# A convolution, attention and routed-expert kernel: filters on a semaphore of their own, filter places filled by three engines, the last logits in two parts

## The reference, cut to what matters

```python
x = x + conv(group_norm(x), bias, up_filter, dn_filter)   # per channel: upsample 2x, 12x12 filter,
                                                          # leaky relu * sqrt(2), 12x12 filter, keep every 2nd
t = tokens(x)                                             # 16 sequences of 1024 tokens, 32 wide
t = t + attention(layer_norm(t), Wq, Wk, Wv)              # causal softmax, one head
t = t + ffn(layer_norm(t), gate_w, gate_b, weight1, weight2)
# ffn: logits of 16 experts per token; softmax over the 1024 tokens of an image; each expert takes its
# 8 strongest tokens, pools them with their weights, two dense layers with gelu, and adds the result
# back to the tokens it took
out = images(t)
```

## Time and profile before

| | |
|---|---|
| median of 3 runs | 413.75 us (411.68 to 414.61) |
| the profiled execution's own time | 406.51 us |
| its span | 404.6 us |
| PE busy | 348.4 us (86%) |
| DVE busy | 310.3 us (77%) |
| ACT busy | 256.4 us (63%) |
| POOL busy | 239.8 us (59%) |
| mean granted TensorE clock | 0.943 |

### The profile page before, as it was taken

One profiled execution on the slowest core, in us unless ns is written; L12 is line 12 of the kernel. 1 busy time (PEld: TensorE's weight loads), 2 busy tenths in 40 slices (PEclk: granted clock), 3 DMA queues, 4 the chain that ended last, 5 costly groups with the idle time before them and its releaser, 6 DMA issues.

```text
span 404.6 us, 7839 instructions
## 1 busy us (share of the span) xinstructions
PE 348.4 (86%) x3046; PEld 260.4 (64%) x3046; DVE 310.3 (77%) x559; ACT 256.4 (63%) x343; POOL 239.8 (59%) x141
## 2 busy tenths in 40 slices
PE   1189998999899999999599999999986887969775
PEld 1068876667587776857477677676764535647574
DVE  2888779786969878699868786986998995765521
ACT  0113454797988959788476778898696888830500
POOL 5314564366679698886734989856497974162000
PEclk9999999999999999999789999999998997998755
DMA  3900000000000000000000000000020000000311
GB/s 105 203 1 2 2 0 2 2 3 0 3 3 2 0 2 3 2 1 2 0 2 2 2 2 2 2 2 2 0 56 0 2 0 25 19 0 20 86 52 53
DMA packets 16033, 6.70 MB, mean 17 GB/s; under 512 B 6735, under 2 KB 15869, under 8 KB 15997
## 3 DMA queue, kind: packets, MB, share of 16 engines
q1 hardware_dynamic: 13280, 5.55, 5.3%
q10 hardware_dynamic: 2717, 0.66, 1.1%
HBM read 3.63 MB, written 2.11 MB: 14 GB/s over the span
## 4 chain that ended last, share of the span: by engine, by line
PE 58%; DVE 15%; ACT 10%; issue 9%; DMA 3%; POOL 2%; SPq 1%; ACTq 1%; DVEq 0%; POOLq 0%
PE psB L874 13%; PE psA L874 11%; PE psB L989 5%; ACT Pp L582 5%; PE psA L974 4%; PE psB L1010 4%; PE psA L1018 3%; PE psA L1054 3%; DVE negmax L739 3%; PE psA L864 3%; PE psA L1032 2%; DVE Pp L393 2%; DVE xin L682 1%; PE psB L992 1%; ACT e L581 1%
## 5 line engine op out<-in xcount | busy, mean ns | idle before, releaser
L393 POOL TENSOR_TENSOR Pp<-e,Pp 128x1024 f16<-128x1024 f32 x45 | 107.3, 2393 | 11.7 <-ACT Pp L582 11.5
L739 DVE TENSOR_REDUCE negmax<-psA 128x1 f32<-128x512 f32 (+7 forms) x128 | 90.7, 749 | 18.5 <-PE psA L977 17.6
L581 ACT ACTIVATE e<-psB 128x1024 f32<-128x1024 f32 (+1 forms) x80 | 76.7, 958 | 9.9 <-PE psB L992 4.5
L582 ACT ACTIVATE Pp<-psB 128x1024 f16<-128x1024 f32 (+1 forms) x80 | 77.0, 963 | 0.0
L874 PE MATMUL psB<-xin,UU 128*128 128x224 f16 (+1 forms) x480 | 56.6, 277 | 1.1 <-ACT Pp L582 0.6
L974 PE MATMUL psA<-zK,yQ 128*128 128x512 f16 (+1 forms) x192 | 49.2, 340 | 9.0 <-DVE uT L759 4.9
L989 PE MATMUL psB<-yQ,zK 128*128 128x512 f16 (+1 forms) x192 | 49.2, 335 | 6.9 <-ACT Pp L582 3.7
L874 PE MATMUL psA<-y,DD 128*128 128x224 f16 (+1 forms) x480 | 55.1, 273 | 0.0
L874 PEld LDWEIGHTS psB<-xin,UU 128*128 128x128 f16 x480 | 47.1, 99 | 9.5 <-ACT oT L586 1.5
L874 PEld LDWEIGHTS psA<-y,DD 128*128 128x128 f16 x480 | 46.7, 98 | 5.5
L489 POOL TENSOR_TENSOR y<-y 128x1024 f16<-128x1024 f32 x16 | 36.7, 2291 | 14.1 <-ACT y L547 14.1
(11 more groups left out here) (157 smaller groups left out, 603.7 us busy)
## 6 DMA issues: line engine op xcount, KB each, us to landing
x_all<-in_x_dram SPq DMA_DIRECT2D x4, 512.0 KB, 4.6
out_dram<-x_all SPq DMA_DIRECT2D x8, 256.0 KB, 2.3
yQ<-rows SPq DMA_DIRECT2D x32, 2.0 KB
Pp<-filter_tables ACTq DMA_DIRECT2D x4, 121.9 KB, 3.3
w_halves<-y SPq DMA_DIRECT2D x12, 32.0 KB, 1.8
cst<-shape_constants SPq DMA_DIRECT2D x1, 326.5 KB, 4.2
y<-in_L_ffn_weight_dram SPq DMA_DIRECT2D x4, 64.0 KB, 1.9
xin<-in_L_ffn_weight_dram SPq DMA_DIRECT2D x1, 256.0 KB, 3.4
```

What stands on the lines that cost most here:

```text
L393: return engine.tensor_tensor(Pp[:, n % 2, 1, o:o + N], e32[:, (NU * n + i) % 3, 0:N], Pp[:, n % 2, 0, o:o + N], ALU.subtract)
L581: nc.scalar.activation(e32[:, m % 3, 0:N], slot(e)[:, 0:N], ACT.Exp)
L582: nc.scalar.activation(Pp[:, n % 2, 0, UOFF[e[2]]:UOFF[e[2]] + N], slot(e)[:, 0:N], ACT.Exp).then_inc(b_drained, 1)
L739: ins = nc.vector.tensor_reduce(negmax[:, n % 2, m - 1:m], s[:, at:at + P * m], X, ALU.max, negate=True)
```

## The change

The opening list becomes `xT 0, U 0, gn_mean 0, U 1, gn_var 0, U 2, normalise 0, image 0, image_low 0`: event `U` is cut in three (sum of neighbours; the two sums; the split) and put between the steps of the group norm, and event `UU` is gone. The four filter places are now filled by SP (r = 0 and 3, two DMAs from SBUF to SBUF), ACT (r = 2) and DVE (r = 1, right behind image 0 of `normalise`). `filters_loaded` counts the two filters only (32) and `bias_loaded` the bias. ACT does a one-element copy before it waits for the filters. On SP the `gb_sb` loads and x group 1 are issued ahead of the wait for `toeplitz_loaded`. At the end the last group's logits are copied and searched for their maxima in two halves of 512 columns, the 16 candidates are reduced to 8, and ACT does a one-element exponential at event `uT` of the last group.

```diff
-FIRST = [("xT", 0), ("gn_mean", 0), ("gn_var", 0), ("U", 0), ("normalise", 0), ("image", 0), ("UU", 0), ("image_low", 0)]
+FIRST = [("xT", 0), ("U", 0), ("gn_mean", 0), ("U", 1), ("gn_var", 0), ("U", 2), ("normalise", 0), ("image", 0), ("image_low", 0)]
...
+        def filter_place(r):
+
+            q = slice(C * r, C * r + C)
+            return (UU[q, :, R - 1 - r:R - 1 - r + NS, :, :].rearrange("p i m q t -> p i (m q t)"),
+                    U_parts[q, :, :, :, :].rearrange("p i m q t -> p i (m q t)"))
... SP
+            for b in range(GB):
+                sp.dma_start(gb_sb[E_ * b:E_ * b + E_, :], gate_b.rearrange("(e a) -> e a", a=1)).then_inc(proj_loaded, 16)
+            sp.dma_start(x_all[:, 1, :].rearrange("p (b a n) -> p b a n", b=GB, a=2), x_tokens[1]).then_inc(x_loaded[1], 16)
             sp.wait_ge(toeplitz_loaded, 16 * R)
-            for g in range(1, G):
+            for g in range(2, G):
...
-            for b in range(GB):
-                sp.dma_start(gb_sb[E_ * b:E_ * b + E_, :], gate_b.rearrange("(e a) -> e a", a=1)).then_inc(proj_loaded, 16)
+            sp.wait_ge(fills_ready, 4)
+            sp.wait_ge(U_split, 2)
+            for r in (0, R - 1):
+                place_to, place_from = filter_place(r)
+                sp.dma_start(place_to, place_from).then_inc(UU_ready, 16)
... ACT
-            act.dma_start(biasr[:, :], bias.rearrange("a h c d -> a (h c d)").broadcast_to([P, H])).then_inc(filters_loaded, 16)
-            act.wait_ge(filters_loaded, 48)
+            act.dma_start(biasr[:, :], bias.rearrange("a h c d -> a (h c d)").broadcast_to([P, H])).then_inc(bias_loaded, 16)
+            nc.scalar.activation(probs[0:1, 0:1], pads[0:1, 0, 0:1], ACT.Copy)
+            act.wait_ge(filters_loaded, 32)
...
+            act.wait_ge(fills_ready, 4)
+            act.wait_ge(U_split, 2)
+            place_to, place_from = filter_place(2)
+            nc.scalar.activation(place_to, place_from, ACT.Copy).then_inc(UU_copied, 1)
...
                 elif name == "logits":
                     if n >= 1:
                         act.wait_ge(route_ready, n)
-                    nc.scalar.activation(lg[:, :], slot(e)[0:GE, :], ACT.Identity, bias=gb_sb[:, 0:1]).then_inc(b_drained, 1)
+                    cut = 0
+                    if n == G - 1:
+                        cut = BANK
+                        act.wait_ge(logits_half, n + 1)
+                        nc.scalar.activation(lg[:, 0:cut], slot(e)[0:GE, 0:cut], ACT.Identity, bias=gb_sb[:, 0:1]).then_inc(lg_half, 1)
+                        act.wait_ge(b_filled, BU[e] + 1)
+                    nc.scalar.activation(lg[:, cut:S], slot(e)[0:GE, cut:S], ACT.Identity, bias=gb_sb[:, 0:1]).then_inc(b_drained, 1)
...
+                elif e == ("uT", G - 1):
+                    act.wait_ge(route_ready, n)
+                    nc.scalar.activation(probs[0:1, 0:1], cst[0:1, 0:1], ACT.Exp)
... DVE
-            dve.wait_ge(filters_loaded, 48)
+            dve.wait_ge(filters_loaded, 32)
...
                         if b in (0, GB - 1):
                             ins.then_inc(xn_ready, 1)
+                        if n == 0 and b == 0:
+                            dve.wait_ge(fills_ready, 4)
+                            dve.wait_ge(U_split, 2)
+                            place_to, place_from = filter_place(1)
+                            nc.vector.tensor_copy(place_to, place_from).then_inc(UU_copied, 1)
... (U in three parts: n == 0 waits for toeplitz_loaded and sums neighbours, n == 1 the two sums, else the split)
                 elif name == "logit_max":
-                    dve.wait_ge(b_drained, BU["logits", n] + 1)
-                    link(nc.vector.max(top8[:, :], lg[:, :]))
+                    if n == G - 1:
+                        dve.wait_ge(lg_half, 1)
+                        nc.vector.max(top16[:, 0:TOP], lg[:, 0:BANK])
+                        dve.wait_ge(b_drained, BU["logits", n] + 1)
+                        link(nc.vector.max(top16[:, TOP:2 * TOP], lg[:, BANK:S]))
+                        link(nc.vector.max(top8[:, :], top16[:, :]))
+                    else:
+                        dve.wait_ge(b_drained, BU["logits", n] + 1)
+                        link(nc.vector.max(top8[:, :], lg[:, :]))
... PE, up 0 and logits
-                        pe.wait_ge(UU_ready, R)
+                        pe.wait_ge(UU_ready, 16 * 2)
+                        pe.wait_ge(UU_copied, 2)
...
+                        if i == 0:
+                            ins.then_inc(logits_half, 1)
```

More of the change, by code:

```diff
@@ L274, in hybrid_kernel @@
         rest = sb("rest", [GE, S])
+        top16 = sb("top16", [GE, 2 * TOP])
         top8 = sb("top8", [GE, TOP])
@@ L336, in hybrid_kernel @@
         w1_high, w1_split, w1_moved = sem("w1_high"), sem("w1_split"), sem("w1_moved")
-        filters_loaded = sem("filters_loaded")
+        filters_loaded, bias_loaded = sem("filters_loaded"), sem("bias_loaded")
         dn_reversed = sem("dn_reversed")
@@ L348, in hybrid_kernel @@
         U_ready = sem("U_ready")
-        UU_ready = sem("UU_ready")
+        UU_ready, UU_copied = sem("UU_ready"), sem("UU_copied")
+        sums_ready, U_split = sem("sums_ready"), sem("U_split")
         stats_ready = sem("stats_ready")
@@ L353, in hybrid_kernel @@
         xin_sum, xin_high, xin_ready = sem("xin_sum"), sem("xin_high"), sem("xin_ready")
-        U_split = sem("U_split")
         y_ready = sem("y_ready")
@@ L368, in hybrid_kernel @@
         u_ready = sem("u_ready")
+        logits_half, lg_half = sem("logits_half"), sem("lg_half")
         lg_max = sem("lg_max")
@@ L473, in image_input @@
                     if g == 0 and i == 0:
-                        pool.wait_ge(filters_loaded, 48)
+                        pool.wait_ge(bias_loaded, 16)
                     v = x_all[:, g, lo:hi].rearrange("p (b h j) -> p b h j", h=H, j=JW)
@@ L529, in _ @@
             act.dma_start(dnE[:, :, :], dn_src).then_inc(dn_toeplitz_loaded, 16)
+            act.wait_ge(fills_ready, 4)
+            act.wait_ge(U_split, 2)
+            place_to, place_from = filter_place(2)
+            nc.scalar.activation(place_to, place_from, ACT.Copy).then_inc(UU_copied, 1)
             for e in EVENTS:
                 name, n = e[0], e[1]
-                if e in BU:
+                if e in BU and e != ("logits", G - 1):
                     act.wait_ge(b_filled, BU[e] + 1)
@@ L575, in _ @@
                     if n == 0:
-                        act.wait_ge(UU_ready, R)
+                        act.wait_ge(UU_ready, 16 * 2)
+                        act.wait_ge(UU_copied, 2)
                         act.wait_ge(a_filled, A["dnT", 0] + 1)
@@ L660, in _ @@
                             ins.then_inc(xn_ready, 1)
-                elif name == "U":
[L663 to L674, removed]
-                    for r in range(R):
-                        q = slice(C * r, C * r + C)
-                        nc.vector.tensor_copy(UU[q, :, R - 1 - r:R - 1 - r + NS, :, :].rearrange("p i m q t -> p i (m q t)"),
-                                              U_parts[q, :, :, :, :].rearrange("p i m q t -> p i (m q t)")).then_inc(UU_ready, 1)
@@ new lines, in _ @@
+                        if n == 0 and b == 0:
[3 more added lines that the diff above has]
+                            nc.vector.tensor_copy(place_to, place_from).then_inc(UU_copied, 1)
+                elif name == "U":
+                    if n == 0:
+                        dve.wait_ge(toeplitz_loaded, 16 * R)
+                        nc.vector.tensor_tensor(upD, upE[:, :, 0:2 * W], upE[:, :, 1:2 * W + 1], ALU.add).then_inc(sums_ready, 1)
+                    elif n == 1:
+                        dve.wait_ge(sums_ready, 1)
+                        nc.vector.tensor_tensor(U[:, :, 0, :], upD[:, 1:2 * NS:2, :], upD[:, 2:2 * NS + 1:2, :], ALU.add).then_inc(U_ready, 1)
+                        nc.vector.tensor_tensor(U[:, :, 1, :], upD[:, 0:2 * NS - 1:2, :], upD[:, 1:2 * NS:2, :], ALU.add).then_inc(U_ready, 1)
+                    else:
+                        dve.wait_ge(U_ready, 2)
+                        high, low = U_parts[:, 0, :, :, :], U_parts[:, 1, :, :, :]
+                        nc.vector.tensor_scalar(high, U, UP_SCALE, None, ALU.mult).then_inc(U_split, 1)
+                        dve.wait_ge(U_split, 1)
+                        nc.vector.scalar_tensor_tensor(out=low, in0=U, scalar=UP_SCALE, in1=high, op0=ALU.mult, op1=ALU.subtract).then_inc(U_split, 1)
```

## The result

| | before | after |
|---|---|---|
| runs of this comparison, us | 405.65, 411.68, 413.75, 414.61 | 401.86, 402.22, 402.43, 402.61 |
| profiled execution, us | 406.51 | 402.22 |
| its span, us | 404.6 | 400.3 |
| mean granted clock | 0.943 | 0.944 |
| PE / DVE / ACT / POOL busy, us | 348.4 / 310.3 / 256.4 / 239.8 | 348.1 / 306.9 / 258.9 / 239.5 |

The ratio of after to before is 0.991, 95% interval 0.9895 to 0.9926: 0.9% faster, where the forecast was 0.8%. The kernel before has executions near 405.7, between 408.9 and 412.1, and near 414 us, which differ in the granted clock (0.943, 0.925 to 0.935, 0.918 to 0.923); the ratio is taken between runs that are comparable in that, which is why it isn't 402.33/412.72, the quotient of the medians.

A forecast was written before the change was run, and what follows sets the result against it. The opening's chain of DMA waits up to up 0 at 24.81 us, and the unoverlapped last logits, were taken as the bounds. Gains of 2.5 and 0.9 sum to 3.4 us: 413.75 - 3.4 = 410.3 us, range 405.5 to 413.6.

The forecast's parts named there:

- so I take the sum from the median: Whole kernel: 3.4 us taken from the median of 413.75, giving 410.3, though the profiled execution was 406.51.
- Filters at 5.6: Opening: on their own semaphore the two filters land at 5.6 us, 0.8 earlier than 6.40.
- Group 1 beside toeplitz: Opening: x group 1, loaded early, delays the toeplitz load by 1.2 us, bounds 0 and 1.4.
- the rival by which they don't: Opening: loads do not disturb each other, toeplitz at 12.4, up 0 gains 3.7 us, time 409.1; chance 0.25.
- Toeplitz at 13.6: Opening: the toeplitz load lands at 13.6 us, against 13.17 before.
- Group 1 is not needed early at all: Opening: loading x group 1 early gains nothing itself, as xT 3 stands ahead of xT 1 on PE.
- DVE last, at 22.0: Opening: DVE's image_low 0 is ready last, at 22.0, 8.3 us plus 0.1 behind toeplitz; up 0 starts at 22.1.
- SP's places at 21.8: Opening: SP's two filter places, issued at 18.8 and 19.3, take 2.5 us and land by 21.8.
- the rival had its place right: Opening: SP's filter places land late, at 25.8; 1.3 us lost, 0.9 gained, time 414.2; chance 0.09.
- Is it carried?: Behind the opening: DVE catches up, tF starts near 36.4 instead of 38.81, and 2.5 us stay gained.
- The last logits 0.9: End of kernel: halved copy and search start the exponential at 377.3 instead of 378.19, 0.9 us gained.
- The clock: PE: another offset makes one more gap with a lower clock, 3.5 us lost, time 413.8; chance 0.08.

The follow-up runs named there:

- experiments 1: Kernel before with only the change of the last logits (halves, 16 candidates, one-element exponential); ratio 1.0016 (0.995 to 1.0081).
- run 3: Kernel after with x group 1 loaded behind the wait for toeplitz again; median 403.07 us, ratio 0.9925.
- run 5: Kernel after with gn_mean moved back in front of U 0; runs from 401.64 to 410.71 us, ratio 0.9927.
- run 2: Kernel before with only the bias counted on its own semaphore; one run at 404.6 us, three from 413.2 to 413.5, no ratio.
- runs 4: Kernel after with x group 3 loaded ahead of group 2 behind toeplitz; median 408.94 us, ratio 1.0061.
- run 6: Kernel after with x group 3 loaded early, ahead of gw_sb, instead of group 1; ratio 1.0083 (1.0055 to 1.0111).
- runs 7: Kernel of run 6 with gb_sb behind toeplitz, one filter place issued by ACT and the order of run 5; ratio 1.0116.
- runs of 9: Kernel of runs 4 with three useless products on PE ahead of dnT 0; eight runs, 403.29 to 412.43 us, ratio 1.0001.
- runs 8: Kernel of runs 7 with five useless products on PE between xT 3 and up 0; median 408.53 us, ratio 1.0028.
- 12: Kernel of runs 8 with useless products in four of PE's gaps; median 400.06 us, ratio 0.9859.
- run 11: Kernel before with useless products in four of PE's gaps; 402.63 to 405.68 us over ten runs, ratio 0.9969.

## Why the prediction was right, and where not

**The size of the change.** Forecast 3.4 us (2.5 and 0.9), measured in the profiles 4.3 (2.99, 0.87, and 0.4 on the way to the last scatter and behind `wT`, within what two executions differ by). In time it is 0.9% of 406, 3.7 us, and 3.15 with filled gaps. Its span was to be 401.2 and was 400.3.

**The time itself.** The 410.3 lies 8 us above the 402.33 measured, and that is below the range's lower end of 405.5. The step that failed is the base: "so I take the sum from the median". The three runs shown were 411.68 to 414.61, the profiled one 406.51, and of the 25 runs of before beside experiments 1 to 4 half were at or under 406.35. The upper ones are before's executions with more time at the lower clock. A sum made against the profiled execution has to stay with it: 406.51 - 3.4 = 403.1. After's four runs all had the clock at 0.944. Whether the change itself avoids the upper levels isn't settled: in run 3, which is after but for one load, nine of ten runs were at the lower level, in run 5 four of ten.

**Step by step.**
- Filters at 5.6: 5.60 (5.43 to 5.74 in the others). Right; no run tests the way there, from the pace of the bias row's packets.
- The table's store. I left it at 1.44. It took 2.04 in after, 1.92 in run 3, and 1.42 in run 2: `gb_sb`'s small loads beside it cost 0.4 to 0.7. This term was missing.
- Group 1 beside toeplitz, forecast 1.2: 4.40 - 3.53 = 0.9 from run 3. Over all profiles the last toeplitz load takes 4.34 to 5.00 with group 1 beside it (five) and 3.43 to 3.60 without (nine), 1.1 on average, so the 1.2 was well sized. The row I judged by (no gap in the engines) was the right one. The queues do disturb each other, so the rival by which they don't, with toeplitz at 12.4, falls. The DMA queues of after, 9.4 to 13.6 us (packets, MB, share of 16 engines):

```profile
q10 hardware_dynamic: 2464, 0.62, 99.3%
q1 hardware_dynamic: 435, 0.21, 17.1%
```

- Toeplitz at 13.6: 13.95. The store adds 0.6, the stretch from the filters' landing to the store's issue 0.2 (5.60 to 6.07, where 6.40 to 6.68 had stood behind the bias), and group 1 takes 0.4 less than I had given it (4.40 for 3.60 + 1.2).
- "Group 1 is not needed early at all", "none" as a gain of its own: wrong. I asked who waits for group 1, and nobody does. The gain is for group 3, which moves up in the queue: run 3 prices it at 1.08 us of `up 0`, net of the 1.0 that toeplitz loses. My "group 3 (about 18.7)" was 19.77, and "both are off the path" with it: `xT 3` ended at 21.84 and not by 20.8.
- DVE last, at 22.0: DVE was ready at 21.34. Behind toeplitz it took 7.4 us for the 8.3 of the sum. POOL's inverse root took 1.31 for 1.79, and the filter place 0.62, not 0.95, although a POOL row of 1.06 stood beside it. `up 0` at 21.90 against 22.1 is therefore a hit by errors that cancel: DVE 0.7 too late, PE's queue 1.0 too early.
- SP's places at 21.8: they landed there, so with 0.1 us to spare; runs 4, 6 and 7, where they are last, show that the rival had its place right. It costs `up 0` 0.2 to 0.6 against after, not the 4 us of its worst bound: in 4 and 6 the places take 2.3 us, in 7 they take 4.0 and 4.6 beside the x loads but are issued earlier.
- Is it carried? Forecast 2.5 of 2.5; 2.91 at `up 0` by the chain (2.7 by the timeline, whose 24.6 for the kernel before the forecast used), 2.99 at `tF`, with the scatter told above. The steady gain down to the end says that it is carried; its size at `tF` is in part luck. D_parts took 1.46 instead of 2.18, as forecast for the split away from POOL, though less than I hoped (0.4).
- The last logits 0.9: 0.77 at the exponential, 0.87 behind `wT`. The halves each cost 0.68 and 0.69 where I had 0.6 and 0.65, and the exponential's table load isn't there; it stands at 362.26, 1.28 long, in ACT's idle time.
- The clock. In this pair the rival did not strike. In the experiments it did, and it is larger than I priced it: not one more gap for 3.5 us, but levels 3 to 6 and 8 us apart of one and the same program. The openings made from after's differ from it by less than 2 us at `tF`, and the kernels' medians by up to 8.

**What stays open.** Why one execution of a kernel has the clock fall at two or three places more than the next; filling four gaps narrows that to 3 us, so gaps are part of it, while no experiment explains which gap brings a fall and which none. The two runs of 9 near 403.5 fit no theory here. The share of the last-logits part in the kernel's time rests on two profiles, not on a timed difference. No run has the new opening alone, so its share of the time isn't timed either. Why the 30 products of `up 0` take 3.87 us in one execution and 5.34 in another of the same opening is open too; the granted clock reads 1.00 there in both.

## What to carry to other kernels

Ask of an early load not only who waits for it, but who stands behind it in the queue; and of a wait that you remove, which others end within a microsecond of it, for a further step gains no more than that. When the profiled execution lies far from the median, predict the difference, look for the levels of the runs, and read the clock's windows before comparing times. If one-microsecond edits change the time by five, close PE's gaps first, in both kernels, and compare then.

## What the runs showed of the hardware that I had not expected

- Four loads of 0.1 KB beside a store of 15 KB lengthen it from 1.42 to 1.92 us (runs 2 and 3; 1.88 to 2.13 in six profiles); with group 3 and `gw_sb` beside it as well, to 3.04 (run 6).
- The same 112 KB from SBUF to SBUF take 2.3 us with the x loads all but through (after) and 3.8 to 4.6 with two of them moving, whichever queue issues them (runs 7, 8 and 12).
- Thirty products at the head of PE's work take from 3.44 to 6.14 us; the shortest came behind useless products, the longest behind 2.69 us of idling (runs 8 and 6), and one and the same opening gives from 3.87 to 5.34 (runs 11 and 1).
- In a program on one core the granted clock goes with levels of one program near 405.7 us (0.943), from 408.9 to 412.1 (0.925 to 0.935) and near 414 (0.918 to 0.923), and 37 useless products in four gaps take most of the spread away (run 11).
